# Second cross attention of a perceiver block: maxima turned by small DMAs, and an earlier start of its loads and first chunks

## The reference, cut to what matters

```python
q = (layernorm(x) @ Wq + bq)        # [2, 256, 16 * 64]
k = (ctx @ Wk + bk)                 # [2, 4096, 16 * 64]
v = (ctx @ Wv + bv)
s = einsum("bqhd,bkhd->bhqk", q, k) / 8
out = softmax(s, -1) @ v            # per head, then Wo, residual, norm
```

## Time and profile before

| | us |
|---|---|
| three executions, median (lowest to highest) | 1978.18 (1962.81 to 1979.93) |
| the profiled execution | 1967.77 |
| its span, first to last instruction | 1965.9 |
| second cross attention: first to last `x_r` of GpSimd | 1155.3 to 1705.2 |
| the attention's block before the first exponential | 1125.4 to 1154.2 |

### The profile page before, as it was taken

The page is one execution under the profiler, slowest core; times in us unless marked ns, Lnnn a source line. Parts: engine busy times, 40 slices in busy tenths (PEclk is TensorE's granted clock), DMA queues, the critical chain, the costliest instruction groups (busy, mean ns, idle before and its releaser), DMA issues. The chain is left out here.

```text
span 1965.9 us, 52765 instructions
## 1 busy us (share of the span) xinstructions
PE 1636.9 (83%) x20036; PEld 961.1 (49%) x20036; DVE 1261.0 (64%) x1971; ACT 984.0 (50%) x1591; POOL 668.2 (34%) x499
## 2 busy tenths in 40 slices
PE   4999999995999999989677368888888888876672
PEld 2445545451334343345433137777776776743442
DVE  3666666554999999836585266666666666236946
ACT  2555555551787878836300135555555555515621
POOL 2330000001111111103210048888888888703400
PEclk8999999996899999985688679999999999887686
DMA  4698979885322222130000715544554543120000
GB/s 158 186 220 236 226 216 223 234 201 143 93 65 66 65 66 65 43 144 1 1 1 1 240 32 140 137 133 131 133 132 125 138 117 94 32 89 1 1 0 11
DMA packets 171211, 213.32 MB, mean 109 GB/s; under 512 B 49928, under 2 KB 144532, under 8 KB 166446
## 3 DMA queue, kind: packets, MB, share of 16 engines
q1 hardware_dynamic: 169776, 210.48, 39.6%
q10 hardware_dynamic: 1280, 0.53, 0.1%
HBM read 123.37 MB, written 87.57 MB: 107 GB/s over the span
## 5 line engine op out<-in xcount | busy, mean ns | idle before, releaser
L1084 POOL TENSOR_TENSOR x_r<-x_p 128x1024 f16<-128x1024 f32 x256 | 477.1, 1893 | 101.9 <-ACT x_p L1056 101.5
L1102 DVE TENSOR_REDUCE x_mx<-a_all 128x2 f32<-128x1024 f32 x256 | 313.4, 1224 | 197.6 <-PE a_all L955 197.6
L1056 ACT ACTIVATE x_p<-s_all 128x1024 f32<-128x1024 f32 x256 | 258.4, 1020 | 139.5 <-PE s_all L939 136.6
L717 ACT ACTIVATE x_p<-s_all 128x1024 f32<-128x1024 f32 x256 | 261.1, 1023 | 49.2 <-PE s_all L627 42.0
L772 DVE TENSOR_REDUCE x_mx<-a_all 128x1 f32<-128x512 f32 x352 | 229.4, 681 | 17.2 <-PE o_all L638 8.8
L986 PE MATMUL o_all<-x_v,x_p 64*128 64x129 f16 x4096 | 218.9, 218 | 11.7 <-issue 8.7
L939 PE MATMUL s_all<-x_q,x_k 64*128 64x256 f16 x3072 | 216.4, 271 | 9.6 <-issue 9.6
L990 PE MATMUL o_all<-x_v,x_r 64*128 64x65 f16 x4096 | 211.6, 190 | 0.6 <-issue 0.6
L986 PEld LDWEIGHTS o_all<-x_v,x_p 64*128 64x128 bf16 x4096 | 192.8, 94 | 22.9 <-issue 17.7
L990 PEld LDWEIGHTS o_all<-x_v,x_r 64*128 64x128 f16 x4096 | 185.9, 95 | 18.6 <-issue 1.3
L939 PEld LDWEIGHTS s_all<-x_q,x_k 64*128 64x128 f16 x3072 | 160.0, 95 | 49.7 <-issue 14.0
(11 more groups left out here) (333 smaller groups left out, 3212.9 us busy)
## 6 DMA issues: line engine op xcount, KB each, us to landing
values<-vst SPq DMA_DIRECT2D x16, 2064.0 KB, 10.6
x_v<-values SPq DMA_DIRECT2D x32, 1032.0 KB, 5.1
keys<-kst SPq DMA_DIRECT2D x32, 1024.0 KB, 7.0
x_k<-keys SPq DMA_DIRECT2D x128, 256.0 KB, 4.6
x_k<-keys SPq DMA_DIRECT2D x192, 64.0 KB, 2.1
values<-vst SPq DMA_DIRECT2D x16, 528.0 KB, 12.8
x_v<-values SPq DMA_DIRECT2D x32, 264.0 KB, 2.6
cf<-in_ctxT SPq DMA_DIRECT2D x16, 512.0 KB, 9.6
```

What stands on the lines that cost most here:

```text
L717: act.activation(prob[g % NP][:], chip.s_ps[g % 2][:].rearrange("p (c q) -> p c q", q=SQ), ACT.Exp, scale=hd ** -0.5).then_inc(p_ready, 1)
L1056: act.activation(prob[g % NP][:], chip.s_ps[g % 2][:].rearrange("p (c q) -> p c q", q=SQ), ACT.Exp, scale=hd ** -0.5).then_inc(p_ready, 1)
L1084: pool.tensor_tensor(rest[g % NP][:], prob[g % NP][:], hi, ALU.subtract).then_inc(rest_done, 1)
L1102: dve.tensor_reduce(mx[a[1] % 2][:, n // 4, 2 * (n % 4):2 * (n % 4) + 2], chip.a_all[:, :].rearrange("p (h c) -> p h c", h=2), AX.X, ALU.m ...
```

## The change

Four things, all around this stage.

1. *The turning.* `x_nm` becomes fp16 and four DMAs (L1064 of the changed kernel) copy its two columns of 128 values into the row `x_qm`, twice for the two halves. ScalarE issues them after exponential 3, where `maximum_columns` stood. `x_mcol`, its identity, TensorE's two products and ScalarE's second copy are gone. `scores` of group 0 waits for the four DMAs (`qm_turned`).
2. *First keys.* The keys of unit (0, 0) are issued in the block of the layer norm.
3. *First queries.* A projection of its own, `project_queries_wide`, writes the first tile of queries (the two heads that the first four units use) ahead of the other seven, loads it again for the four units, then issues the values and the other keys, and writes the seven tiles without waiting for them to land. The wait stands at SP's start in the attention (`written`). ScalarE's 16 loads are gone. `qh` and `ql` now live in the attention's buffers.
4. *Two chunk buffers.* In the two units before the first, every second `pair` goes to `o_all`, which is not yet in use, and waits for the maximum before last only. Scores 0 and 1 of the first unit come after the pairs of steps 5 and 6 instead of before those of 6 and 7.

```diff
+    def loads(self, sp):
+        self.load_keys(sp, 0, 0)
...
+def project_queries_wide(chip, tag, weight, bias_q, buffers):
...
+                sp.dma_start(bq[:], bias_q).then_inc(loaded, 16)
+                qd = buffers.q_dram.rearrange("h (m p) t -> h p m t", p=P)
+                sp.wait_ge(hi, 1)
+                sp.dma_start(qd[0, :, 0], qh[:, 0, :]).then_inc(buffers.first_written, 16)
+                sp.wait_ge(lo, 1)
+                sp.dma_start(qd[1, :, 0], ql[:, 0, :]).then_inc(buffers.first_written, 16)
+                buffers.load_keys(sp, 0, 1)
+                sp.wait_ge(buffers.first_written, 32)
+                for u in range(4):
+                    buffers.load_queries(sp, 0, u)
+                buffers.load_values(sp, 0, 0)
+                for u in range(2, 4):
+                    buffers.load_keys(sp, 0, u)
+                    buffers.load_values(sp, 0, u - 1)
+                buffers.load_values(sp, 0, 3)
+                sp.wait_ge(hi, MT)
+                sp.dma_start(qd[0, :, 1:], qh[:, 1:, :]).then_inc(buffers.written, 16)
+                sp.wait_ge(lo, MT)
+                sp.dma_start(qd[1, :, 1:], ql[:, 1:, :]).then_inc(buffers.written, 16)
...
-        nm = [chip.sb(f"{tag}_nm{i}", [P, 2], F32, scope) for i in range(2)]
-        mcol = [chip.sb(f"{tag}_mcol{i}", [P, 2, 2, 64], F16, scope) for i in range(2)]
+        nm = [chip.sb(f"{tag}_nm{i}", [P, 2], F16, scope) for i in range(2)]
...
+        def chunk_banks(u, g):
+
+            return chip.o_all if not real(u) and g % 2 else chip.a_all
...
+                sp.wait_ge(buffers.written, 32)
                 with sp.Fori(0, PAIRS - 1) as it:
...
-                        pe.wait_ge(qm_done, nth(u, 1, 1))
+                        pe.wait_ge(qm_turned, nth(u, 64, 64))
...
-                    if real(u) or g + 8 * u[1] > -14:
+                    into = chunk_banks(u, g)
+                    if real(u):
                         pe.wait_ge(pair_done, nth(u, GR, 14 + g))
-                    if g == 5 and (real(u) or u[1] == -1):
-                        pe.wait_ge(qm_done, nth(u, 1, 2))
+                    elif g + 8 * u[1] > -13:
+                        pe.wait_ge(pair_done, nth(u, GR, 13 + g))
...
-                        if g == 4 and (real(u) or u[1] == -1) and ahead(u, 1):
-                            negated_maxima(u, ahead(u, 1))
+                        elif u[1] == -1 and g in (5, 6):
+                            scores((0, 0), g - 5)
...
-                for w in range(W):
-                    buffers.load_queries(act, 0, w)
...
-                def maximum_columns(a):
+                def turn(a):
                     i = a[1] % 2
                     act.wait_ge(nm_done, nth(a, 1, 1))
-                    act.activation(mcol[i][:, :, :, 0], nm[i][:].unsqueeze(2).to_broadcast([P, 2, 2]), ACT.Copy).then_inc(mcol_done, 1)
-
-                def queries(a):
-                    act.wait_ge(qm_ready, nth(a, 1, 1))
-                    act.activation(qm[a[1] % 2][:], chip.a_all[:, 0:SQ], ACT.Copy).then_inc(qm_done, 1)
+                    for h in range(2):
+                        for t in range(2):
+                            act.dma_start(qm[i][64 * h:64 * h + 1, t * P:(t + 1) * P], nm[i][:, t:t + 1]).then_inc(qm_turned, 8 * 2)
...
                         if g == 3 and ahead(u, 1):
-                            maximum_columns(ahead(u, 1))
-                        if g == 6 and ahead(u, 1):
-                            queries(ahead(u, 1))
+                            turn(ahead(u, 1))
```

More of the change, by code:

```diff
@@ L410, in project_queries @@
         w = weight.w
[L411 removed]
         qh = chip.sb(f"{tag}_qh", [P, MT, TOK], F16, scope)
         ql = chip.sb(f"{tag}_ql", [P, MT, TOK], F16, scope)
[L414 removed]
+        ready, hi, lo, out = (chip.sem(f"{tag}_{n}") for n in ("rdy", "hi", "lo", "out"))
         with nc.Block() as block:
@@ L417, in _ @@
             def _(sp):
-                if bias_q is not None:
-                    sp.dma_start(bq[:], bias_q).then_inc(loaded, 16)
-                if early is not None:
-                    early(sp)
                 qd = q_dram.rearrange("h (m p) t -> h p m t", p=P)
@@ L835, in load_values, with _ @@
         eng.dma_start(self.v[w][:], vd.rearrange("h p c e -> p (h c) e")).then_inc(self.v_loaded[w], 16)
+def project_queries_wide(chip, tag, weight, bias_q, buffers):
+    nc = chip.nc
+    MT = NH * 64 // P
+    with ExitStack() as scope:
+        w, qh, ql = weight.w, buffers.qh, buffers.ql
+        bq = chip.sb(f"{tag}_bq", [P, MT], F32, scope)
+        loaded, ready, hi, lo = (chip.sem(f"{tag}_{n}") for n in ("ld", "rdy", "hi", "lo"))
+        with nc.Block() as block:
+            @block.sync
+            def _(sp):
+                sp.dma_start(bq[:], bias_q).then_inc(loaded, 16)
[17 more added lines that the diff above has]
+                sp.dma_start(qd[1, :, 1:], ql[:, 1:, :]).then_inc(buffers.written, 16)
+            @block.tensor
+            def _(pe):
+                pe.wait_ge(weight.loaded, 16)
+                for m in range(MT):
+                    if m >= 4:
+                        pe.wait_ge(lo, m - 3)
+                    for k in range(KT):
+                        last = pe.matmul(chip.banks[m % 4], w[:, k, m * P:(m + 1) * P], chip.xnT[:, k, :],
+                                         start=(k == 0), stop=(k == KT - 1))
+                    last.then_inc(ready, 1)
+            @block.scalar
+            def _(act):
+                act.wait_ge(loaded, 16)
+                for m in range(MT):
+                    act.wait_ge(ready, m + 1)
+                    act.activation(qh[:, m, :], chip.banks[m % 4], ACT.Identity, bias=bq[:, m:m + 1]).then_inc(hi, 1)
+            @block.vector
+            def _(dve):
+                for m in range(MT):
+                    dve.wait_ge(hi, m + 1)
+                    dve.scalar_tensor_tensor(out=ql[:, m, :], in0=chip.banks[m % 4], scalar=bq[:, m:m + 1],
+                                             in1=qh[:, m, :], op0=ALU.add, op1=ALU.subtract).then_inc(lo, 1)
@@ L2121, in perceiver @@
                 buffers = WideCrossBuffers(chip, "x1", inner, queries[1], *scratch[1])
-                def early(sp):
-                    buffers.load_keys(sp, 0, 0)
-                    for w in range(1, 4):
-                        buffers.load_keys(sp, 0, w)
-                        buffers.load_values(sp, 0, w - 1)
-                    buffers.load_values(sp, 0, 3)
                 with ExitStack() as innermost:
                     wq = Prefetch(chip, "q1", innermost, t["a1q"])
-                    layer_norm(chip, "ln3", after=[wq])
-                    project_queries(chip, "q1", wq, t["a1bq"], 64, queries[1], early)
+                    layer_norm(chip, "ln3", after=[wq, buffers])
+                    project_queries_wide(chip, "q1", wq, t["a1bq"], buffers)
                 cross_attention_wide(chip, "x1", buffers, att)
```

55 lines of the change are left out of this document (16 added, 39 removed).

## The result

The changed kernel takes 2007.8 us (median of 4, 1992.5 to 2014.5); the kernel before, run beside it, 1977.2 us (median of 4). The ratio is 1.016, 95% interval 1.010 to 1.022. I had forecast 1974 us in a range of 1935 to 2006: the sign was wrong, and the time lies 2 us outside the range. Rival B, "the issues are dear", had worked out 2008 us; how much of that agreement is luck is said further down.

A forecast was written before the change was run, and what follows sets the result against it. TensorE was busiest (83% of the span), with a chain through ScalarE's exponential 4 and output copy ending last in the loop. Terms -1 - 3 - 8 + 8 = -4 us from the median 1978.2 gave 1974 us, range 1935 to 2006.

The forecast's parts named there:

- Rival B: Loop: dear issues make ScalarE's queue the bound at exponential 4; 1989 us at 0.62 us each, 2008 at 0.76; chance 0.14.
- The chain: Loop: exponential 4, output copy, then values(u, 0) end last; ScalarE work put ahead reaches TensorE one for one.
- my formula: Loop stall per unit: hold less 0.16 us in 17 units, less 1.39 in 14; mean 1.28 us for a 2.0 us hold.
- part 1: Loop, maxima turned by DMA: four ScalarE issues at 0.5 us stall TensorE 1.28 us a unit against 1.0 saved: +8 us.
- my upper end: Loop, turning by DMA: four issues taking 2.47 us a unit, mean stall 1.76 us, +23 us.
- The old turning's saving: Loop: two TensorE products and their wait removed, 1.0 us of TensorE a unit.
- rival A: Cheap issues, 0.34 us or less: loop -9, or -31 where the new stall vanishes; 1957 or 1935 us; chance 0.31.
- Pieces: Turning's issues: the number of pieces hardly counts (341 ns for 128, 392 ns for 1024).
- rival C: Loop: turned maxima land late, 11 us after the maxima; TensorE waits 2 to 3 us a unit; about 2035 us; chance 0.08.
- Part 2: Before the attention loop, first keys and queries: SP free earlier, -1 us; gap until TensorE begins, -3 us.
- Part 3: Prologue, two chunk buffers: reductions 1.24 us apart; first product to exponential 0 16.9 us instead of 24.7: -8 us.
- The sum: Forecast total -1 - 3 - 8 + 8 = -4 us; its terms outside the loop are -12 us.

The follow-up runs named there:

- turn_late: Changed kernel with the four issues moved behind exponential 4 and the output copy: 1981.6 us, ratio 1.006.
- turn_sp: Changed kernel with the four issues made by SP, ahead of its value load, instead of by ScalarE: 1953.8 us, ratio 0.991.
- sp_filled: Changed kernel with the four issues on SP and three idle copies a unit holding ScalarE's queue where it had issued: 2011.9 us, ratio 1.019.
- turn_half: Changed kernel with two of the four issues a unit left out, so the maxima reach one half of the keys: 1961.0 us, ratio 0.995.
- old_turn: Changed kernel with the old turning (copy, two products, copy) put back, early loads and two chunk buffers kept: 1956.9 us, ratio 0.993.
- one_chunk: Changed kernel with one chunk buffer in the prologue again: 2011.3 us, ratio 1.018.
- turn_two: Changed kernel with two ScalarE issues a unit, each carrying both columns, the matmul reading the row with a stride: 1963.5 us, ratio 0.993.
- turn_rows: Changed kernel with four issues that each copy one contiguous row of zeros instead of the maxima: 2004.9 us, ratio 1.020.

## Why the prediction was wrong

**The chain was read rightly.** That exponential 4, the output copy and `values(u, 0)` end last, and that what ScalarE puts ahead of them goes through to TensorE, is what turn_late (the wait goes back to 3.5 us), turn_sp and sp_filled show. "One for one" holds beyond a slack that I had taken somewhat too small: my formula (17 units with 0.16 us of cover, 14 with 1.39) gives 70 us for holds of 2.96 us and 16 us for those of 1.13 us; the waits were 63.8 and, in turn_half, 9.8 us.

**The step that failed** is in part 1: "I take 0.5 us each, 2.0 us". Measured: 0.74 us each in the mean, 2.96 us a unit. With it the stall, taken as 1.28 us in each of 31 units or 40 us, came to 63.8. I had halved the distance between ScalarE's 618 ns and SP's 341 ns, on the thought that 128 partitions and no DRAM address make it cheap. Both SP and ScalarE take 0.59 to 0.62 us (medians) for such an issue, and ScalarE took 618 ns for a query load, so ScalarE's own row was the nearer one. But it isn't enough: the mean lies above the median, with single issues up to 1.7 us, and my upper end, 2.47 us and +23, was therefore no bound.

**What the sum put at nothing.** The matmuls that both kernels share took 16.2 us more, with the granted clock down from 0.99 to 0.96, and TensorE's wait put down to issue before the products of `x_qm` grew by 9.6 us (14.5 to 24.1). The whole loop then adds up: 63.8 - 25.3 (the old turning's wait of 18.6 and 6.7 of matmuls) + 16.2 + 9.6 is 64.3; smaller waits, above all L939's and L986's for issue, gave back the rest down to 57.0. Rows of the changed kernel show how a stall costs clock. After one wait for the copy TensorE ran at a granted clock of 0.50, the lower of its levels, 1.2 GHz:

```profile
1628.20 0.29 PE L1027 MATMUL o_all<-x_v,x_p 64*128 64x129 f16 x2 [3.78 <-ACT x_lsb L1072]
```
```profile
1628.20:1633.00 4.80, 4.80 (x82) 4.07 (x84) 1.14 (x1) 1.70 (x2) 3.41 (x3) 0.50 0.04 9
```

And after a wait that is put down to issue, TensorE being idle for most of five microseconds, it ran at 0.67, that is mostly at the lower level:

```profile
1611.00:1616.00 5.00, 0.17 (x2) 0.14 (x4) 0.25 (x1) 0.07 (x1) 3.06 (x2) 0.71 0.54 111
1616.00:1622.00 6.00, 6.00 (x106) 4.54 (x104) 2.34 (x2) 2.05 (x2) 1.97 (x2) 0.67 0.01 3
```

The price in clock doesn't follow the idle time alone: in turn_late TensorE was idle for 102.3 us at a clock of 0.98, in turn_sp for 74.0 us at 0.97.

**Rival B's 2008 us** is in part luck. Its working (delay 3.04, less 0.7 of cover, less 1.0 saved, 31 times) gives +41 for the loop and has neither the clock nor the wait for issue in it, while it starts from the median of the kernel before, 10 us above the profiled execution against which the loop rose by 57.

**The old turning's saving** was taken as 1.0 us a unit, 31 us in all; the earlier trace rows give 0.9. L966 and its wait are gone in every run with DMAs, but no run shows the saving in its time. In turn_sp, where the new stall is gone as well, the loop is 558.2 us against 549.8 before and 565.0 in old_turn, and TensorE's idle time is 74.0 us against 75.1 in old_turn: what left with L966 came back as the wait for issue (37.3 us against 18.1 in old_turn). The ratios of the two runs lie some 4 us apart, less than their intervals. So rival A's "-31 where the new stall vanishes" was wrong too.

**Pieces.** That the number of pieces hardly counts for the issue was right (611 against 622 ns). The Trainium skill (Perfetto Trace Analysis, 'DMA Instruction — HWDGE (DVE, Sync)') says that an issue's span ends only after all of its descriptors are generated; between 32 and 144 packets an issue these runs show hardly any growth.

**Landing (rival C)** was hidden in the changed kernel, but not as forecast. I had the last row land 4.2 to 7.2 us after the maxima; it landed after 5.9 to 9.3, with a median of 8.5. It stayed hidden probably because the stall delayed its reader too; turn_late shows the rows exposed.

**Part 2** was forecast at -1 and -3. From the bias's issue SP was free 34.6 us later against 37.7 us for the block's start before, and the wait for queries became 1.15 us: about -3 and -3. **Part 3** was forecast at -8: 24.7 to 18.0 is -6.7, of which one_chunk shows 5.7 to be the second buffer. The reductions stood 1.13 us apart, less than the 1.24 I took, while the issues (2.51) and the landing took more. The sum, -12.7 against -12, was right, helped by errors of opposite sign in the parts, and old_turn bears it out with 14 us on the medians.

## What to carry to other kernels

A DMA issue is an instruction of the engine that issues it: at 0.6 us each, and here a mean of 0.9 for the third and fourth of a unit, four of them are three exponentials' worth of ScalarE's queue. Before moving work from an engine to DMAs, look for what stands behind the issues in that queue and who waits for it, price them by the same engine's rows and not by a thought on their shape, and give them to the queue that has time; here the same DMAs from SP turn +1.6% into -0.9%. Then ask what the move was for: with the old turning the new prologue alone reaches -0.7%, so the work that TensorE was rid of gave next to nothing. A stall that is put in every round can also cost clock, so its price can be more than its length.

## What was not expected

- The price of issues isn't proportional to their number. Against turn_sp, by ratios and by medians, two issues a unit on ScalarE (1.13 us a unit) cost 7 to 8 us in turn_half and 5 to 10 in turn_two, four (2.96 us a unit) cost 50 to 54 us: exponential 4 had 0.8 to 0.9 us of slack, and only the third and fourth issue are stretched.
- Landing depends on how a row is cut. 128 pieces of two bytes landed in 4.0 us with four issues a unit and in 3.6 us with two (turn_half); 128 pieces of four bytes, also two issues at the same place, landed in 2.0 us (turn_two), and a contiguous row in 2.2 us (turn_rows).
- In the fast versions another stall has grown: once in each pass of the loop over four units, which points to its back edge, TensorE stands up to 5.3 us, put down to issue, and its next matmuls run at the lower clock (0.61 us for the pair of matmuls that takes 0.39 otherwise). From turn_sp, TensorE in order of time and the total:

```profile
1225.44 0.61 PE L997 MATMUL s_all<-x_qm,x_ones 64*128 64x512 f16 x2 [5.30 <-issue]
```
```profile
PE s_all L997 <- issue: 37.3, 12, 5.3
```

The kernel before has 14.5 us of it, the changed kernel 24.1. What lengthens it was not tried; it is the next thing to look at in turn_sp.
